# Memory/SwiGLU block of an eight-stage transformer kernel: another filling order, joined time-step tables, gates turned amid the up products

## The reference, cut to what matters

```python
# attention half, on the layer-normed x
Bm, Cm = x @ W_B + b_B, x @ W_C + b_C
dt = softplus((x @ W_dt1 + b_dt1) @ W_dt2 + b_dt2)      # W_dt1 128x32, W_dt2 32x128
phi = cumsum(omega_base * dt); content = Bm * x
retrieved = Cm * (cumsum(content*cos(phi))*cos(phi) + cumsum(content*sin(phi))*sin(phi))
y = retrieved @ W_out + b_out + D * x
# feed-forward half, on the layer-normed result: 16 experts of 64, top 4 out of 2 of 4 groups, one shared expert of 128
a = silu(x @ w1[e]) * (x @ w3[e]);  y = sum_e c[t,e] * (a @ w2[e]) + (silu(x @ ws1) * (x @ ws3)) @ ws2
```

## Time and profile before

| | |
|---|---|
| median of 3 runs | 1577.16 us (1574.89 to 1578.33) |
| profiled execution | 1576.58 us, span 1574.8 us |
| TensorE busy, whole span | 1288.2 us (82%) |
| VectorE busy | 1029.2 us (65%) |
| ScalarE busy | 802.3 us (51%) |
| GpSimd busy | 535.9 us (34%) |
| mean granted TensorE clock | 0.885 |
| the stage here | 683.7 to about 1056 us: filling to 789 (first up), steps 0 to 7 to 1053 |

### The profile page before, as it was taken

One profiled execution on the slowest core, in us unless ns is written; L12 is line 12 of the kernel. 1 busy time (PEld: TensorE's weight loads), 2 busy tenths in 40 slices (PEclk: granted clock), 3 DMA queues, 4 the chain that ended last, 5 costly groups with the idle time before them and its releaser, 6 DMA issues. The chain is left out here.

```text
span 1574.8 us, 21830 instructions
## 1 busy us (share of the span) xinstructions
PE 1288.2 (82%) x6696; PEld 718.4 (46%) x6696; DVE 1029.2 (65%) x2781; ACT 802.3 (51%) x1606; POOL 535.9 (34%) x668
## 2 busy tenths in 40 slices
PE   5899999999997128935589989875899997689898
PEld 1223333333333118932345555643466755577633
DVE  7778888888853665635987785323467653566486
ACT  2467777776783004527646543312455452456554
POOL 3342343343210006358455345330112112333046
PEclk7799999999998558975699999985799998699999
DMA  5211111111105302210023333321132131000001
GB/s 151 57 49 30 52 48 41 42 52 52 32 12 157 70 1 66 59 36 24 8 55 70 72 76 55 76 39 34 58 112 62 62 107 57 30 2 1 1 21 34
DMA packets 80774, 81.15 MB, mean 52 GB/s; under 512 B 19899, under 2 KB 64139, under 8 KB 80659
## 3 DMA queue, kind: packets, MB, share of 16 engines
q1 hardware_dynamic: 77327, 74.06, 18.0%
q0 software_dynamic: 2304, 4.72, 1.3%
q10 hardware_dynamic: 1028, 0.98, 0.2%
HBM read 64.32 MB, written 13.92 MB: 50 GB/s over the span
## 5 line engine op out<-in xcount | busy, mean ns | idle before, releaser
L933 DVE TENSOR_REDUCE a_nm<-a_aps 128x1 f32<-128x512 f32 x512 | 333.5, 686 | 75.2 <-PE a_aps L698 75.2
L897 ACT ACTIVATE a_prob<-a_sps 128x512 f32<-128x512 f32 x512 | 271.4, 597 | 114.6 <-PE a_sps L710 113.6
L698 PE MATMUL a_aps<-a_K,a_Q 96*128 96x512 bf16 x512 | 195.1, 401 | 13.0 <-DMA a_K<-k_parts 12.7
L710 PE MATMUL a_sps<-a_Q,a_K 99*128 99x512 bf16 x512 | 156.2, 385 | 1.2 <-ACT a_prob L897 1.2
L1402 POOL TENSOR_TENSOR p_h<-p_sl,p_t 128x512 f32<-128x512 f32 x72 | 105.5, 1484 | 143.3 <-ACT p_sl L1542 74.3
L719 PE MATMUL a_ops<-a_prob,a_Vg 128*32 128x512 f32 x1024 | 136.9, 609 | 0.0
L698 PEld LDWEIGHTS a_aps<-a_K,a_Q 96*128 96x128 bf16 x512 | 50.3, 98 | 140.7 <-DVE a_nm L933 90.4
L1542 ACT ACTIVATE p_sl<-p_up_a 128x512 f32<-128x512 f32 x72 | 42.9, 597 | 112.5 <-PE p_up_b L1432 112.5
L1928 POOL TENSOR_TENSOR c_h<-c_h,c_G 128x512 f32<-128x512 f32 x24 | 31.7, 1325 | 181.0 <-ACT c_h L2114 163.8
L407 POOL CAST a_ms<-a_mr 16x128 bf16<-16x128 f32 x32 | 9.0, 280 | 243.0 <-ACT a_mr L855 243.0
L1432 PE MATMUL p_up_b<-x_normT,p1w_w 128*128 128x512 f32 x144 | 76.4, 613 | 7.9 <-DVE p_t L1650 7.6
(11 more groups left out here) (571 smaller groups left out, 2702.2 us busy)
## 6 DMA issues: line engine op xcount, KB each, us to landing
p_G<-gates_by_expert SPq DMA_DIRECT2D x32, 512.0 KB, 6.9
c_G<-choice_rows SPq DMA_DIRECT2D x32, 512.0 KB, 6.4
a_Q<-q_parts SPq DMA_DIRECT2D x192, 32.0 KB
a_K<-k_parts SPq DMA_DIRECT2D x31, 96.0 KB
q_parts<-a_partsq SPq DMA_DIRECT2D x7, 384.0 KB, 2.8
k_parts<-a_partsk SPq DMA_DIRECT2D x7, 384.0 KB, 2.8
token_outputs<-m0e_y SPq DMA_DIRECT2D x40, 64.0 KB, 1.5
m0w_w<-in_L_ffn_W SPq DMA_DIRECT2D x1, 2048.0 KB, 9.4
```

Of the source, the lines that this page charges most:

```text
L698: nc.tensor.matmul(aps[n % 3][:, :], Q[0:MAX, head, q * P:(q + 1) * P], K[0:MAX, head, :], start=True, stop=True).then_inc(a_ready, 1)
L710: nc.tensor.matmul(sps[(NS * u + k) % 3][:, :], K[0:KB, head, k % TC * P:(k % TC + 1) * P], Q[0:KB, head, :], start=True, stop=True).then_ ...
L897: nc.scalar.activation(prob[u % 2][:, k // TC, k % TC, :], sps[n % 3][:, :], ACT.Exp).then_inc(p_done, 1)
L933: nc.vector.tensor_reduce(nm[u % 2][:, s:s + 1], aps[n % 3][:, :], AX.X, ALU.max, negate=True).then_inc(a_used, 1)
```

## The change

- In the filling (s < 0) every engine has an order of its own, and `continue`s past the old one. TensorE: turn_gates, turn_second, turn_first, logits, time step, outer, input_gates. ScalarE: keep_gates, second_normal, copy_first, copy_second, softplus_parts, gate_exponentials, (trig for chunk 0), Exp and Ln, second_root, trig, first_root. VectorE: second_rstd, memory 0 to 3, shift_logits, choose, memory 4 to 8, add_memory, phase, first_rstd, add_back.
- The first chunk: `add_back(0)` before the loop, its first normalisation on VectorE (`normal_here`).
- The tables W1 and W2 are multiplied once on chip (`join_tables`) with their bias, so the time step takes one 128x128 product (`steps_of_time`), read by `softplus_parts` from `up_b[0]`.
- The gates are turned after unit MID = 5 of the ups of the step before, into `ops` and not `up_b[0]`; the shared expert becomes the first unit (`expert`). The first unit no longer waits for the gates of its chunk.

The diff, cut to its core (waits and declarations that follow from it are left out; the three new orders are TensorE's, ScalarE's and VectorE's):

```diff
+        expert = lambda j: (j + NP) % NW
+        MID = 5
...
             def first_normal(c):
-                pool.wait_ge(rstd1_done, c + 1)
-                wait(pool, x1_turned, c - 1)
-                for k in range(TC):
-                    last = normal(c, xn1, net.rstd, k)
-                last.then_inc(xn1_done, 1)
+                if c > 0:
+                    pool.wait_ge(rstd1_done, c + 1)
...
                 if j == 0:
                     pe.wait_ge(xT2_done, min(c + 2, B))
                     pe.wait_ge(z_read, min(c + 5, B))
-                    pe.wait_ge(t1_done, min(c + 5, B))
                     pe.wait_ge(shifted, min(c + 2, B))
-                    pe.wait_ge(gT_done, c + 1)
...
             def turn_gates(c):
                 pe.wait_ge(gate_done, c + 1)
-                pe.wait_ge(t1_done, min(c + 5, B))
-                wait(pe, gT_done, c)
-                for k in range(TC):
-                    last = nc.tensor.transpose(up_b[0][0:E, k * P:(k + 1) * P], gate[:, TC * c + k, :], net.ident[:, :])
+                pe.wait_ge(o_added, min(c + 2, B))
+                for k in range(TC):
+                    last = nc.tensor.transpose(ops[0:E, k * P:(k + 1) * P], gate[:, TC * c + k, :], net.ident[:, :])
...
+            def steps_of_time(c):
                 pe.wait_ge(xT1_done, c + 1)
...
+                wait(pe, z_read, c)
+                if c == 0:
+                    pe.wait_ge(W12_done, 2)
+                nc.tensor.matmul(up_b[0][:, :], W12[:, :], net.xT[:, c * S:(c + 1) * S], start=True, stop=True).then_inc(z_ready, 1)
+
+            def join_tables():
+                nc.tensor.transpose(yps[0:T1, 0, :], W1[:, :], net.ident[:, :]).then_inc(W1_turned, 1)
+                pe.wait_ge(W1T_done, 1)
+                nc.tensor.matmul(yps[:, 1, :], W1T[:, :], W2[:, :], start=True, stop=True)
+                nc.tensor.matmul(yps[:, 2, 0:8], W2[:, :], b1[:, :].to_broadcast([T1, 8]), start=True, stop=True).then_inc(W12_ready, 1)
...
+                if s < 0:
+                    if here(s + 1):
+                        turn_gates(s + 1)
+                    if here(s + 2):
+                        turn_second(s + 2)
+                    if here(s + 5):
+                        turn_first(s + 5)
+                    if here(s + 2):
+                        logits(s + 2)
+                    if here(s + 5):
+                        steps_of_time(s + 5)
+                    if here(s + 3):
+                        outer(s + 3)
+                    if here(s + 4):
+                        input_gates(s + 4)
+                    continue
                 for j in range(NW):
                     if here(s):
                         up(s, j)
+                    if here(s + 1) and j == MID:
+                        turn_gates(s + 1)
...
+                if s < 0:
+                    if here(s + 1):
+                        keep_gates(s + 1)
+                    if here(s + 2):
+                        second_normal(s + 2)
+                    if here(s + 5):
+                        copy_first(s + 5)
+                    if here(s + 2):
+                        copy_second(s + 2)
+                    if here(s + 5):
+                        softplus_parts(s + 5)
+                    if here(s + 2):
+                        gate_exponentials(s + 2)
+                    if s + 4 == 0:
+                        trig(s + 4)
+                    if here(s + 5):
+                        softplus_exp(s + 5)
+                        softplus_log(s + 5)
+                    if here(s + 3):
+                        second_root(s + 3)
+                    if here(s + 4) and s + 4 > 0:
+                        trig(s + 4)
+                    if here(s + 7):
+                        first_root(s + 7)
+                    if s == -1:
+                        nc.scalar.preload_act_table(ACT.Silu)
+                    continue
...
+            add_back(0)
             for s in steps:
+                if s < 0:
+                    if here(s + 2):
+                        second_rstd(s + 2)
+                    for j in range(4):
+                        if here(s + 3):
+                            memory(s + 3, j)
+                    if here(s + 2):
+                        shift_logits(s + 2)
+                        choose(s + 2)
+                    for j in range(4, NW):
+                        if here(s + 3):
+                            memory(s + 3, j)
+                    if here(s + 3):
+                        add_memory(s + 3)
+                    if here(s + 4):
+                        phase(s + 4)
+                    if here(s + 6):
+                        first_rstd(s + 6)
+                    if s + 6 == 0:
+                        normal_here(s + 6)
+                    if 0 < s + 7 < B:
+                        add_back(s + 7)
+                    if s == -1:
+                        add_back(B - 1)
+                    continue
```

More of the change, by code:

```diff
@@ L1386, in first_normal @@
             def first_normal(c):
-                pool.wait_ge(rstd1_done, c + 1)
-                wait(pool, x1_turned, c - 1)
-                for k in range(TC):
-                    last = normal(c, xn1, net.rstd, k)
-                last.then_inc(xn1_done, 1)
+                if c > 0:
+                    pool.wait_ge(rstd1_done, c + 1)
+                    wait(pool, x1_turned, c - 1)
+                    for k in range(TC):
+                        last = normal(c, xn1, net.rstd, k)
+                    last.then_inc(xn1_done, 1)
                 pool.wait_ge(xn1_done, c + 1)
@@ L1439, in down @@
                 for j in range(NW):
-                    last = nc.tensor.matmul(yps[:, k, :], h[c % 2][:, j, k * P:(k + 1) * P], w2[:, j, :],
+                    last = nc.tensor.matmul(yps[:, k, :], h[c % 2][:, j, k * P:(k + 1) * P], w2[:, expert(j), :],
                                             start=(j == 0), stop=(j == NW - 1))
@@ L1447, in outer @@
                 wait(pe, o_added, c)
+                wait(pe, gT_done, c - 1)
                 for q in range(TC):
@@ L1464, in turn_first @@
                 pe.wait_ge(xn1_done, c + 1)
-                wait(pe, z_read, c)
+                wait(pe, xT1_done, c)
                 for k in range(TC):
@@ L1564, in copy_second @@
                 nc.scalar.activation(net.xT[:, c * S:(c + 1) * S], up_a[1][:, :], ACT.Copy).then_inc(xT2_done, 1)
[L1566 to L1569, removed]
             def softplus_parts(c):
-                act.wait_ge(t2_ready, c + 1)
+                act.wait_ge(z_ready, c + 1)
                 wait(act, phi_done, c - 1)
-                nc.scalar.activation(rz[c % 2][:, :], up_a[0][:, :], ACT.Relu, bias=b2[:, :])
+                nc.scalar.activation(rz[c % 2][:, :], up_b[0][:, :], ACT.Relu, bias=b12[:, :])
                 act.drain()
-                nc.scalar.activation(az[:, :], up_a[0][:, :], ACT.Abs, bias=b2[:, :]).then_inc(z_read, 1)
+                nc.scalar.activation(az[:, :], up_b[0][:, :], ACT.Abs, bias=b12[:, :]).then_inc(z_read, 1)
             def softplus_exp(c):
@@ L1720, in add_back, with normal_here @@
                 measure_chunk(c, bst0, bst0_done, stat0_done)
+            def normal_here(c):
+                v.drain()
+                for k in range(TC):
+                    n = TC * c + k
+                    last = ts(xn1[c % 2][:, k, :], net.x[:, n, :], net.stat[:, n, 0:1], net.rstd[:, n:n + 1],
+                              ALU.subtract, ALU.mult)
+                last.then_inc(xn1_done, 1)
             def first_rstd(c):
@@ L1800, in _ @@
                     measure_output(s - 1)
-                if s < 0 and here(s + 2):
-                    shift_logits(s + 2)
                 if here(s + 4):
                     phase(s + 4)
-                if s >= 0 and here(s + 2):
+                if here(s + 2):
                     shift_logits(s + 2)
@@ L1810, in _ @@
                     choose(s + 2)
-                if here(s + 8):
-                    add_back(s + 8)
 def causal_and_gelu(nc, net, d):
```

61 lines of the change are left out of this document (25 added, 36 removed).

## The result

The changed kernel took 1586.61 us (median of 5, 1585.22 to 1588.87) against 1577.13 for the kernel before: a ratio of 1.007, 95% interval 1.005 to 1.0089, so about 11 us by the ratio and 9.5 by the medians. The forecast was +3.9 us, 1581.0, in a range of 1571 to 1587. The direction held and the time lies at the upper edge of the range; 9.5 us came where 3.9 were forecast.

What follows compares the result with a forecast made beforehand. VectorE was taken to set the end of the filling, TensorE's gaps the steps 0 to 7. Filling +12 (-14.3 and +26.5) and steps -8.1 gave +3.9 us: 1580.5 for the profiled execution, median 1581.1, range 1571 to 1587.

Steps and rivals of the forecast that it cites:

- Part 1, the head start: Filling: chunk 0's normalisation on VectorE, joined tables and earlier trig(0) start memory(0) sooner, -14.3 us.
- Part 2, the waits: Filling: VectorE's new order waits on other engines, 28.2 us in sum against 2.9 before; +26.5 us net.
- outer: Filling: VectorE idle before add_memory for outer at half clock, 3.7 us twice and 4.0 in step -3.
- exponentials: Filling: VectorE idle before choose, as gate_exponentials stands behind softplus_parts, 4.4 us twice.
- logits: Filling: VectorE idle before shift_logits, 3.8 us, and 4.2 in step -1 where gates are copied too.
- Part 3, the steps: Steps 0 to 7: no product waits for gates and the 32-row product goes, -8.1 us in sum.
- the stretch from the first transposes to the downs: Steps 0 to 7, TensorE: 9.67 us becomes 8.8 without the 32-row product, -0.9.
- The slower case: GpSimd's normalisations fall on memory and choose and stretch VectorE; steps give back only 4: +12.5, 1589 us; chance 0.15.
- The covered case: Filling's stalls are covered, or outer and logits come earlier; -8 to -12, 1567 to 1569 us; chance 0.15.
- The case of late gates: Gates late despite the turn in the ups, since SP must write, reread and spread them; judged hardly likely.
- The clock case: Clock rises in the filling, half the links at full speed: filling +6, steps -8.1, so 1575 us; chance 0.2.
- the four links at full clock: Filling: logits, transposes, matmul and outer at full clock lose 1.1, 1.1, 1.0 and 1.7, some 4.6 us a step.

Runs made afterwards that it cites:

- a_old_fill: Changed kernel with the old order of the filling on every engine, without chunk 0's head start; joined tables and new steps stay: 0.994 of the kernel before.
- f_choose_last: Changed kernel; in the filling VectorE takes the old order with choose last, ScalarE takes trig ahead of second_root, head start stays: 0.9897 of the kernel before.
- d_warm: Changed kernel with two extra products, results overwritten, in TensorE's gap before the second transposes in steps 0 to 5: 1.0033 of the kernel before.

## Why the prediction was off

**Part 1, the head start: -14.3 forecast, -12.8 measured** (`memory(0)` after the stage's start). Its parts: 4.8 for the joined tables and 8.0 for the rest (a_old_fill against f_choose_last). Right in kind, 1.5 too large. The transposes of chunk 1 started at 711.99 and not at 710.0, and `trig(0)` followed. The join of the tables, put at nothing, is borne out: it was done by 686.2, and ScalarE was not asked again before 694.

**Part 2, the waits: right in kind and nearly in size.** Forecast 28.2 us, measured 25.2, each kind where it was put: outer 11.6 (forecast 11.4), exponentials 8.8 (8.8), logits 4.8 (8.0). The logits were over-counted mainly because the first half of `memory` took 5.8 us (742.04 to 747.85) instead of the 4.6 of rows 3, and so covered more: one of its products (`p_cs`, 743.60) took 1.77 us instead of 0.68, beside GpSimd's addition of the bias (743.57 to 744.83). Filling forecast +12, measured +12.6. That this is so close is partly luck: the head start was 1.5 us smaller than forecast, and the stretch behind it grew by 25.4 and not by 26.5, which makes up for 1.1 of it. The choice of half clock for every link was right: the granted clock was 0.55 and 0.59 in the last two steps.

**Part 3, the steps: -8.1 forecast, +1.6 measured. This step of the prediction failed.** What it said of the work was right: no product waits for its gates any more, and the ups of step 1 take 17.1 us (16.8 forecast, 18.15 before). With the clock held up, d_warm's steps take 246.5 us, where the forecast's sum is 254.9 - 8.1 = 246.8. The mis-sized term is the stretch from the first transposes to the downs, taken as 8.8 us at full clock. It measured 11.41 us in step 0 and 10.15 in step 1, where the clock fell, and 8.56 in step 2, where it did not; d_warm has 8.54 in all three. The forecast wrote that 2.9 us would pass until `second_normal` is there, and did not ask what the clock does after them, though for the filling it had asked exactly that; only in step 0 did it allow 0.6 us for half clock. By the table against d_warm, the changed kernel lost 3.0 us in step 0, 1.6 in step 1, 1.3 in step 3, 1.2 in step 4 and 2.7 in step 5, together 9.8 us, where the forecast missed 9.7. The agreement of d_warm with the forecast's sum is a little flattered: its steps 4 and 5 came out 0.6 and 1.1 us below the forecast, since the added products also took away losses that the kernel before itself had there, while steps 1 to 3 saved 0.2 to 0.9 us less than forecast. In steps 3 to 5 the gap of 2.4 was there before as well; step 3 of the kernel before got through it at full clock, and its step 4 did not.

**The rivals.** The slower case named GpSimd's normalisations beside VectorE as its mechanism; the amount was near (+12.5 for +11), the mechanism was not it. In steps -2 and -1 of the changed kernel each took 3.49 us (at 740.00 and 773.20), more than half of it ahead of `memory`, where the kernel before shows 5.25. And f_choose_last needs 65.0 us from `memory(0)` to the product, as before. The 3.65 us that the prediction calls a normalisation alone were not alone either: VectorE added and took statistics beside it, from 701.44 to 703.45. The covered case did not come in this order, as VectorE waited its 25.2 us, but f_choose_last shows that another order covers them. The case of late gates did not come. The clock case had the clock rising in the filling; it stayed down there, and fell where I had it up. Two sums in these cases are off, without touching the forecast: the four links at full clock save 4.9 us and not 4.6, and -8 to -12 gives 1565 to 1569, not 1567 to 1569.

**The signs.** Those of the filling came as written: `memory(0)` at 720.7 (719), the first product at 811.2 (810) without a wait for DMA, waits of 2.2 to 4.4 us, a clock of 0.55 and 0.59 (0.66 from 720 to 742). Step 1 took 35.4 us and not 33.5, and the steps saved under 4, which was named as a sign of being wrong. The reason named with it, ups bound by VectorE or GpSimd, was not it: the ups came out at 17.1 us, 0.3 over forecast.

**Left open.** Why the same gap costs the clock in one step and not in the next; the runs show only that it did not in any step where the gap was split or filled. Nor do they show whether the idle time alone counts: in step 1 of the changed kernel 4.5 us lie between the last up and the next product (863.54 to 868.03), and the work in between is two sets of transposes; no run takes these out.

## What to carry to other kernels

When a hand-written order puts several short operations of one engine in a row, each fed by another engine, add up the waits: here three kinds, 25.2 us, ate a head start of 12.8, and putting long independent work between question and answer gave all of it back. A product that is removed from a gap, or moved behind it, is not a saving until you know what the clock does after the longer gap. Measure parts of a change apart: this one held some 13 us of gain in its tables and the first chunk's head start, up to 8 in its steps, which the clock took away, and 25 of loss in VectorE's order.

## What the runs showed that was not expected

- A gap of 2.27 us on TensorE was followed by products at 1.71 us from start to start instead of 0.86, for 3 to 6 us. Split by a product into idle stretches of 0.73 and 0.39 us, the gap left the clock at 1.00. Two needless products, 1.7 us of work, in each of six steps made the stage 10 us shorter in the profiled execution, and the kernel 6 to 8.5 us by the ratios.
- The table of steps repeats to 0.1 us between different kernels as long as the clock does the same (33.8, 31.7, 26.6, 27.9), and jumps by 1.2 to 3 us where it does not.
- The stage began between 681.1 and 693.4 us in kernels whose earlier stages are the same. Marks counted from the stage's start were far steadier: the first product came 126.9 to 127.0 us after it in all four executions with the changed kernel's filling.
